# A transformer stage on one core: head pairs on row tiles of TensorE, projections by products of short parts, and a fixed order for each engine

## The chip, the cores and the metric

The kernel runs on one core of one Trainium2 chip. A core has five engines that run side by side, each through its own list of instructions in a fixed order, and synchronised by semaphores: TensorE (matrix products; PE in the profile, its weight loads PEld), VectorE (DVE), ScalarE (ACT), GpSimd (POOL), and SyncE (SP), which here issues all DMAs. The metric is the time of one execution in microseconds (us).

## The reference, cut to what matters

The kernel computes six blocks on `x` (4 x 256 x 256): cross attention, convolutional attention, a local transformer, cross attention, gated linear attention, and a mixture of experts. The change touches the third, a transformer of 6 layers whose attention looks back at most 64 tokens:

```python
DIM, DEPTH, HEADS, DIM_HEAD, WINDOW, INNER = 256, 6, 16, 64, 64, 1024
def attn_layer(x, Wqkv, qs, ksc, Wo):
    q, k, v = jnp.split(x @ Wqkv, 3, -1)                     # then split into 16 heads of 64
    q = l2norm(q) * qs
    k = l2norm(k) * ksc
    q = q * cos * scale + rotate_half(q) * sin * scale
    k = k * cos * inv + rotate_half(k) * sin * inv
    out = local_attention(q, k, v)                           # softmax(8 q k) v, j <= i <= j + 64
    return out @ Wo
def ffn_layer(x, g, bln, W1, b1, W2, b2):
    xn = (x - mu) / jnp.sqrt(var + 1e-05) * g + bln
    a, gate = jnp.split(xn @ W1 + b1, 2, -1)
    return a * jax.nn.gelu(gate, approximate=False) @ W2 + b2
for i in range(DEPTH):                                       # shift_tokens: half of the features one token later
    x = attn_layer(shift_tokens(x), Wqkv[i], q_scale[i], k_scale[i], Wo[i]) + x
    x = ffn_layer(shift_tokens(x), ln_g[i], ln_b[i], W1[i], b1[i], W2[i], b2[i]) + x
```

## The kernel before, in words

Each block is a stage (`Cross`, `Conv`, `Local`, `Gated`, `Experts`). The stage `Local` works on jobs: job j = 4 l + b is layer l of batch b, 24 in all, each with 256 tokens as two tiles of 128. A job has three parts, made as generators of steps:

- `front`: `features` (transpose the shifted x, L1803), then for q and k (sec 0 and 1), two tiles and two halves of 512 columns `proj` (L1811, two four-byte products), `sumsq` and `norm` (square on ScalarE L1612, sums on VectorE L1698, the power -1/2 on GpSimd L1579), the rotation on VectorE (L1684 to L1688) with an addition on GpSimd (L1572), `scale_k` (L1714), `turn` (transpose q or k, L1823, copied by ScalarE L1622 to L1626), and `values` (L1831, copied by L1631).
- `back`: attention by the class `Attention`, head by head. `front` there adds the mask (L965) and the scores (L967) in one bank for both query tiles; VectorE takes row maxima (L1005) and scales them (L1009), ScalarE the exponentials (L1038), VectorE (L1016, L1019) and GpSimd (L1026) divide; `turn` transposes the weights (L979 and L977, the latter a product with 64 output rows), ScalarE copies them (L1045); `apply` multiplies a pair of heads with the values (L990, two column tiles of 64), copied by L1476. q is kept twice, with zeros in the rows of the other head, so that 128 rows are multiplied. Then `wo` (L1855).
- `gated`: the feed-forward part, `fs`, `f_stats`, `f_scale`, `ft` (L1862), `w1` (L1871) with `gate` (ScalarE L1644, VectorE L1765), `w2` (L1881).

`order` interleaves the front of job n, the back of job n-1 and the gated part of job n-2 by `even`, which spreads each evenly over the same number of ticks. The one resulting list, `plan`, is the order of all five engines: each walks through it and does its own share of every step. Banks: 2 for scores, 2 for transposed weights, 1 for apply, 3 taken in turn by the steps `features`, `proj`, `turn`, `values`, `wo`, `ft`, `w1`, `w2`; TensorE waits for a bank of the three until its last user is copied out (`lt_gen_free`). The weights of q and k have two buffers, so a layer's are loaded during the layer before it.

In the stage `Experts`, products of four-byte numbers are made differently: each operand is split into a high part of short precision and the rest (type fp32r), and three products, high x high, high x low, low x high (`PARTS`), stand for one (L2414, L2429). In `Cross` the scores of two heads use two row tiles (L844, L856: 50 and 48 rows at rows 0 and 64).

## Time and profile before

| | |
|---|---|
| three runs | median 5052.75 us (5047.61 to 5063.53) |
| the profiled execution | 5055.65 us, span 5053.7 us |
| granted TensorE clock, mean | 0.970 |
| TensorE busy | 4552.4 us, 90% |
| VectorE, ScalarE, GpSimd busy | 3254.5, 2900.7, 1877.3 us |
| stage `Local` | about 1337 to 3337 us of the span |

A group or timeline row names line, engine, operation, output<-inputs, the shapes, and how many (x). A product of full four-byte numbers leaves two records in the trace, one of short parts a single record. A matmul's duration includes the time until its result is out, so what it costs in a row of others is read from start to start. "idle before <-" tells what ended an engine's idle time; "issue" is time for which the profile shows no cause.

### The profile page before, as it was taken

What the parts mean: (1) busy time and instruction counts of PE and PEld (TensorE: products, weight loads), DVE (VectorE), ACT (ScalarE), POOL (GpSimd) and SP (SyncE); (2) the same over time, 40 slices, a digit from 0 to 9 for tenths busy, and PEclk for the clock granted to TensorE, in tenths of its full rate; (3) what the DMA queues carried; (4) which work ended last, traced back from release to release, by engine and by line L of the source; (5) the groups of instructions that cost most, each with busy time, mean ns of one, the idle gap of its engine ahead of it and who ended that gap; (6) DMA issues with size and microseconds to landing.
All of it is one profiled execution on the core that took longest, in us unless ns stands there. A gap on an engine that the chain in (4) does not pass through costs nothing. (4 is left out here: it accounts for less than half of the span.)

```text
span 5053.7 us, 86339 instructions
## 1 busy us (share of the span) xinstructions
PE 4552.4 (90%) x32008; PEld 3054.5 (60%) x32008; DVE 3254.5 (64%) x7543; ACT 2900.7 (57%) x5798; POOL 1877.3 (37%) x1876
## 2 busy tenths in 40 slices
PE   5889998989699999999999999948999999759999
PEld 3555555547456666666666666635555555448888
DVE  5677777767565655656565565536777777575555
ACT  3666666668455656566565665615666666523332
POOL 3222232125454544445454444313222222025554
PEclk8999999999899999999999999979999999879999
DMA  6655555400200010100101000046556555111110
GB/s 136 128 102 106 106 113 107 77 23 1 70 23 15 24 33 12 53 13 14 44 12 53 5 23 24 4 98 136 111 102 113 107 106 89 24 49 48 47 48 22
DMA packets 189934, 305.64 MB, mean 60 GB/s; under 512 B 19736, under 2 KB 109752, under 8 KB 187832
## 3 DMA queue, kind: packets, MB, share of 16 engines
q1 hardware_dynamic: 189520, 300.13, 27.1%
q8 instruction: 259, 4.24, 0.4%
q14 instruction: 155, 1.27, 0.1%
HBM read 215.81 MB, written 73.40 MB: 57 GB/s over the span
## 5 line engine op out<-in xcount | busy, mean ns | idle before, releaser
L707 DVE TENSOR_REDUCE xa_m_part<-xa_ring 128x1 f32<-128x512 f32 x2048 | 1319.4, 686 | 505.8 <-PE xa_ring L856 491.5
L633 ACT ACTIVATE xa_ex<-xa_sc 128x1024 f32<-128x1024 f32 x1024 | 991.6, 1022 | 109.8 <-PE xa_sc L844 95.0
L856 PE MATMUL xa_ring<-xa_ks,xa_q_base 48*128 48x512 f32 x2048 | 517.8, 497 | 183.2 <-DVE xa_m_part L707 129.7
L870 PE MATMUL xa_pv<-xa_ex,xa_vs 128*17 128x256 f32 x8192 | 549.4, 386 | 4.2 <-issue 4.2
L856 PEld LDWEIGHTS xa_ring<-xa_ks,xa_q_base 48*128 48x128 f32 x2048 | 200.9, 185 | 515.3 <-DVE xa_m_part L707 433.6
L1572 POOL TENSOR_TENSOR lt_r_qk<-lt_r_qk,lt_t_rot 128x512 f32<-128x512 f32 x192 | 243.5, 1269 | 695.1 <-DVE lt_t_rot L1688 691.2
L1038 ACT ACTIVATE lt_p<-lt_bank,lt_stat,lt_rq 128x128 f32<-128x128 f32 (+1 forms) x768 | 366.2, 482 | 216.4 <-DVE lt_stat L1009 211.2
L844 PE MATMUL xa_sc<-xa_q_base,xa_ks 50*128 50x256 f32 x4096 | 423.1, 302 | 26.8 <-ACT xa_k L605 5.8
L844 PEld LDWEIGHTS xa_sc<-xa_q_base,xa_ks 50*128 50x128 f32 x4096 | 347.1, 187 | 117.4 <-ACT xa_vs L620 24.4
L1026 POOL TENSOR_SCALAR lt_p<-lt_p,lt_stat 128x192 f32<-128x192 f32 x384 | 339.9, 889 | 203.4 <-DVE lt_stat L1016 203.4
L2414 PE MATMUL moe_bank<-moe_xp,moe_wp 128*128 128x512 f32 x1536 | 373.3, 392 | 5.9 <-POOL moe_wp L2242 4.2
L1811 PE MATMUL lt_bank<-lt_wqk,lt_xt 128*128 128x512 f32 x768 | 366.2, 600 | 0.7 <-ACT lt_xt L1605 0.7
L555 POOL CAST xa_kp<-xa_k 128x512 fp32r<-128x512 f32 (+1 forms) x144 | 85.3, 592 | 653.3 <-ACT xa_k L613 311.7
L1579 POOL TENSOR_TENSOR lt_nrm<-lt_nrm,minus_half 128x16 f32<-128x16 f32 x96 | 280.5, 2922 | 122.6 <-DVE lt_nrm L1705 121.5
L2414 PEld LDWEIGHTS moe_bank<-moe_xp,moe_wp 128*128 128x128 f32 x1536 | 281.5, 189 | 59.9 <-issue 4.3
L870 PEld LDWEIGHTS xa_pv<-xa_ex,xa_vs 128*17 128x17 f32 x8192 | 189.1, 97 | 202.0 <-issue 62.7
L1612 ACT ACTIVATE lt_t_sq<-lt_bank 128x512 f32<-128x512 f32 x192 | 114.7, 597 | 296.2 <-DVE lt_t_rot L1688 296.2
L2277 ACT ACTIVATE moe_sg<-moe_bank 128x512 f32<-128x512 f32 x128 | 76.5, 598 | 341.1 <-PE moe_bank L2414 341.1
L979 PE MATMUL lt_bank<-ident,lt_p 128*128 128x128 f32 x768 | 240.5, 313 | 34.5 <-issue 34.5
L1871 PE MATMUL lt_bank<-lt_ft,lt_w 128*128 128x256 f32 x1152 | 262.1, 381 | 1.2 <-DVE lt_ft L1753 1.2
L2248 POOL TENSOR_TENSOR moe_hp<-moe_hh,moe_hp 128x512 fp32r<-128x512 f32 x128 | 166.0, 1297 | 256.9 <-ACT moe_hp L2255 256.9
L1005 DVE TENSOR_REDUCE lt_stat<-lt_bank 128x1 f32<-128x128 f32 (+1 forms) x768 | 210.7, 316 | 52.6 <-PE lt_bank L967 52.4
(283 smaller groups left out, 8962.8 us busy)
## 6 DMA issues: line engine op xcount, KB each, us to landing
xa_ks<-keys SPq DMA_DIRECT2D x384, 256.0 KB, 9.3
keys<-xa_kp SPq DMA_DIRECT2D x128, 512.0 KB, 3.8
xa_cx<-in_ctx_t SPq DMA_DIRECT2D x64, 512.0 KB, 4.6
lt_wqk<-in_lt_wqkv SPq DMA_DIRECT2D x6, 2048.0 KB, 9.0
lt_w<-in_lt_w SPq DMA_DIRECT2D x6, 1536.0 KB, 7.1
xa_q_base<-xa_m_rows SPq DMA_DIRECT2D x512, 2.0 KB
moe_w<-in_moe_wg SPq DMA_DIRECT2D x64, 128.0 KB, 2.1
moe_w<-in_moe_wu SPq DMA_DIRECT2D x64, 128.0 KB, 2.3
```

What stands on the lines that cost most here:

```text
L633: act.activation(x.ex[:, n % x.NE, :, :], x.sc[n % 2][:, :, :], ACT.Exp).then_inc(*x.ex_done.one())
L707: dve.tensor_reduce(x.m_part[:, i % 2, qt, h, ch:ch + 1], x.bank(n + odd), AX.X, ALU.max).then_inc(*x.dve_out.one())
L844: mm = pe.matmul(x.sc[n % 2][:, 2 * odd + pair, :], x.ks[unit % x.NU][rows, 2 * (g % 2) + pair, kt * P:(kt + 1) * P], x.q_base[rows, 2 * g ...
L856: pe.matmul(x.bank(n + odd), x.q_base[rows, pair, b * S + qt * P:b * S + (qt + 1) * P], x.ks[unit % x.NU][rows, pair % 4, ch * 512:(ch + 1 ...
L870: mm = pe.matmul(x.pv[32 * j:32 * j + x.VW, :], x.vs[:, i % x.NV, kt, 4 * g + j, :], x.ex[:, n % x.NE, 2 * (j % 2) + j // 2, :], start=(kt ...
L1026: pool.tensor_scalar(sv, sv, self.stat[:, n % 5, 3, 1:2], None, ALU.mult).then_inc(*self.div_pool.one())
L1038: act.activation(self.p[:, n % 5, at], s[:, at], ACT.Exp, bias=t3[:, 1, q:q + 1], scale=st.scale_of(b, h, slice(q, q + 1)) if st.scale is ...
L1572: pool.tensor_tensor(out, out, self.t_rot[:, t, :], ALU.add).then_inc(*self.rot_add.one())
L1579: pool.tensor_tensor(n[:, 2, :], n[:, 1, :], c.minus_half[:, 0:H], ALU.pow).then_inc(*self.rnorm.one())
L1811: mm = pe.matmul(bank[:, :], self.xt[:, par, k, tile * P:(tile + 1) * P], self.wqk[:, l % 2, k, col:col + 512], start=(k == 0), stop=(k == ...
L1871: mm = pe.matmul(bank[:, gate * S:(gate + 1) * S], self.w1[:, k, gate * FFP + m * P:gate * FFP + (m + 1) * P], self.ft[:, k, :], start=(k ...
L2414: mm = pe.matmul(self.banks[2 * (n % 2) + j][:, :], self.wp[:, wpart, i, j, k * FI:(k + 1) * FI], self.xp[:, xpart, k, at], start=(m == 0) ...
```

## The change

- Attention by a new class `Band`, on pairs p of heads. The scores of the even head use rows 0 to 63, of the odd one rows 64 to 127 (`st.q[rows, ...]`), so q is kept once, without zeros. The mask has 384 columns. Three banks for scores (of which a pair takes two), one for transposed weights, one for apply. Maxima of a head come from one instruction, scale and reciprocal of a pair from one.
- Projections and values by `PARTS`, six products in place of two. The weights come in 6 chunks of 512 columns (`raw`), are copied by ScalarE and subtracted by VectorE (`split`), into single buffers `wqk`, `wval`; the features are split in the same way.
- The attention of all jobs is one run of pairs: the transposes (`set_keys`) of a pair stand two pairs behind its scores, apply three, across jobs. `values` and `wo` stand together after the third pair. The gated part is that of job n-3.
- ScalarE, VectorE and GpSimd no longer follow `plan`. `order_of` sorts the steps for each of them by when TensorE reaches them by a table (`PE_TIME`), plus a delay (`LATER`), but before the step that needs them.

Core of the diff:

```diff
+    def pe_front(self, pe, on, st, p):
+        for odd in range(2):
+            on.wait_ge(self.exp_done, 2 * (2 * p + odd - 3) + 2)
+            pe.matmul(self.scores(2 * p + odd)[:, 0:2 * self.BLOCK], self.c.ident_bf[:, :], st.mask[:, :],
+                      start=True, stop=False)
+        j, hp = divmod(p, H // 2)
+        for q in range(2):
+            for odd in range(2):
+                rows = slice(64 * odd, 64 * odd + 64)
+                at = slice(self.BLOCK * q, self.BLOCK * q + self.KEYS[q])
+                mm = pe.matmul(self.scores(2 * p + odd)[:, at], st.q[rows, j % 2, hp, q * P:(q + 1) * P],
+                               st.kt[rows, j % 2, hp, self.FIRST[q]:self.FIRST[q] + self.KEYS[q]],
+                               start=False, stop=(q == 1))
...
+    def pe_turn(self, pe, on, n):
+        on.wait_ge(self.div_dve, 2 * (n // 2) + 2)
+        on.wait_ge(self.div_pool, n // 2 + 1)
+        on.wait_ge(self.t_out, n)
...
-    scale = None
+    PE_TIME = dict(features=0.5, proj=1.5, values=1.5, turn=0.5, attend=1.0, set_keys=0.6, apply=0.6, wo=3.4,
+                   ft=0.5, w1=1.7, w2=2.6)
...
-            self.at = Attention(c, "lt", ctx, (self.banks[0:2], self.banks[2:4], self.banks[4]), 4, 2, 1, WINDOW)
+            self.at = Band(c, "lt", ctx, self.banks[0:3], self.banks[4], self.banks[3])
...
+    def order_of(self, engine):
...
+        for step in self.plan:
+            key = ends[step] + self.LATER[engine].get(step[0], 0.0)
+            rank = self.RANK.index(step[0]) if step[0] in self.RANK else len(self.RANK)
+            for need in self.needed_by(step):
+                if need in begins:
+                    key = min(key, begins[need] - 0.01 * (len(self.RANK) + 1 - rank))
+            keys[step] = key
+        return sorted(self.plan, key=lambda step: keys[step])
...
-        for n in range(len(jobs) + 2):
-            parts = [(part(*jobs[n - lag]), steps, late) for lag, (part, steps, late) in
-                     enumerate(((self.front, 24, 0), (self.back, 23, 0), (self.gated, 17, 0.1)))
-                     if 0 <= n - lag < len(jobs)]
+        for n in range(len(jobs) + 2):
+            parts = [(part(*jobs[n - lag]), steps, 0) for lag, part, steps in
+                     ((0, self.front, 20), (1, self.back, 38), (3, self.gated, 21))
+                     if 0 <= n - lag < len(jobs) - (lag != 1)]
...
+            elif kind == "split":
+                n, = a
+                _, parts, last = self.chunk(n)
+                on.wait_ge(self.raw_in[n % 2], n // 2 + 1)
+                if n >= self.CHUNKS:
+                    on.wait_ge(self.gen_full, self.use[last] + 1)
+                act.activation(parts[:, 0, :, :], self.raw[:, n % 2, :, :],
+                               ACT.Copy).then_inc(*self.w_high.one())
...
-                    mm = pe.matmul(bank[:, :], self.xt[:, par, k, tile * P:(tile + 1) * P],
-                                   self.wqk[:, l % 2, k, col:col + 512], start=(k == 0), stop=(k == KC - 1))
+                    for xpart, wpart in PARTS:
+                        mm = pe.matmul(bank[:, :], self.xt[:, par, xpart, k, tile * P:(tile + 1) * P],
+                                       self.wqk[:, wpart, k, col:col + 512], start=(m == 0),
+                                       stop=(m == 3 * KC - 1))
+                        m += 1
```

TensorE before, at the start of a job's attention: L965 is a mask, L967 scores, L1811 a projection; bank0 and bank1 hold scores.

```order
L965 MATMUL lt_bank0<-lt_mask,ident_bf 128x320 [waits at_exp_done,lt_rq_done,lt_gen_free2]
L967 MATMUL lt_bank0<-lt_kt,lt_q_even 128x128
L967 MATMUL lt_bank0<-lt_kt,lt_q_even 128x192
L1811 MATMUL lt_bank6<-lt_wqk,lt_xt 128x512 [waits lt_gen_free1]
L1811 MATMUL lt_bank6<-lt_wqk,lt_xt 128x512
L965 MATMUL lt_bank1<-lt_mask,ident_bf 128x320 [waits at_exp_done]
L967 MATMUL lt_bank1<-lt_kt,lt_q_odd 128x128
L967 MATMUL lt_bank1<-lt_kt,lt_q_odd 128x192
```

TensorE now, around the same place (L1391 to L1394 the transposes of one head's weights, L1328 masks, L1335 scores, L2034 a projection, line numbers of the changed kernel):

```order
L1391 MATMUL lt_bank4<-ident,lt_p 128x128 [waits at_t_out]
L1392 MATMUL lt_bank4<-ident,lt_p 64x128
L1394 MATMUL lt_bank4<-ident,lt_p 128x128
L1328 MATMUL lt_bank2<-lt_mask,ident_bf 128x384 [waits at_exp_done,lt_gen_free1,lt_gen_free0]
L1328 MATMUL lt_bank0<-lt_mask,ident_bf 128x384 [waits at_exp_done]
L1335 MATMUL lt_bank2<-lt_kt,lt_q 128x128
L1335 MATMUL lt_bank0<-lt_kt,lt_q 128x128
L1335 MATMUL lt_bank2<-lt_kt,lt_q 128x192
L1335 MATMUL lt_bank0<-lt_kt,lt_q 128x192
L2034 MATMUL lt_bank7<-lt_wqk,lt_xt 128x512 [waits w_low,lt_gen_free2]
L2034 MATMUL lt_bank7<-lt_wqk,lt_xt 128x512 x5
```

The products of the two heads alternate between two banks, the transposes of weights all go to the one bank4 and wait there for ScalarE's copy of the head before (at_t_out), and between transposes and the next pair no other work stands.

ScalarE now, in the same stretch (L1362 exponentials, L1400 copies of transposed weights, L1836 of apply, L1819 of a turn):

```order
L1400 ACTIVATE lt_pt<-lt_bank4 128x384 [waits at_t_full]
L1819 ACTIVATE lt_kt<-lt_bank7 128x4x128 [waits lt_gen_full]
L1362 ACTIVATE lt_p,lt_stat<-lt_bank0,lt_stat,lt_rq 128x128 [waits at_max_done]
L1362 ACTIVATE lt_p,lt_stat<-lt_bank0,lt_stat,lt_rq 128x192
L1362 ACTIVATE lt_p,lt_stat<-lt_bank1,lt_stat,lt_rq 128x128
L1362 ACTIVATE lt_p,lt_stat<-lt_bank1,lt_stat,lt_rq 128x192
L1836 ACTIVATE lt_ot<-lt_bank3 128x256 [waits at_pv_done]
L1400 ACTIVATE lt_pt<-lt_bank4 128x384 [waits at_t_full] x2
L1836 ACTIVATE lt_ot<-lt_bank3 128x256 [waits at_pv_done]
L1362 ACTIVATE lt_p,lt_stat<-lt_bank2,lt_stat,lt_rq 128x128 [waits at_max_done]
```

Four exponentials now stand together where there were two, with the copies before and behind them.

## Rows read from the trace of the kernel before

**Rows 1.** The page: each engine's busy time, its share of the span, instructions.
```profile
PE 4552.4 (90%) x32008; PEld 3054.5 (60%) x32008; DVE 3254.5 (64%) x7543; ACT 2900.7 (57%) x5798; POOL 1877.3 (37%) x1876
```
**Rows 2.** Busy time by stretch: stretch, length, engines (x records), clock, DMA share, GB/s.
```profile
1528.00:1606.00 78.00, 75.96 (x387) 51.10 (x387) 46.42 (x140) 49.38 (x125) 37.10 (x31) 1.00 0.02 6
...
1684.00:1762.00 78.00, 75.93 (x393) 50.89 (x393) 47.23 (x140) 47.50 (x120) 35.28 (x29) 1.00 0.07 20
```
**Rows 3.** Line 1803, features: durations min/median/max in ns, first and last start.
```profile
L1803 PE MATMUL lt_bank<-ident,lt_xs x48: 272/273/421, 1365.1 to 3144.3; 128*128 128x128 f32 x48
```
**Rows 4.** Waits of TensorE, 1336 to 3345 us: total us, times, longest.
```profile
PE lt_bank L979 <- issue: 34.5, 24, 1.5
```
**Rows 5.** Timeline of TensorE, 1760 to 1780 us: start us, us, instruction.
```profile
1763.41 1.88 PE L1811 MATMUL lt_bank<-lt_wqk,lt_xt 128*128 128x512 f32 x4
1765.13 0.30 PE L965 MATMUL lt_bank<-lt_mask,ident_bf 128*128 128x320 bf16 x1
...
1765.91 0.87 PE L990 MATMUL lt_bank<-lt_pt,lt_v 128*64 128x256 f32 x8
1766.71 0.33 PE L979 MATMUL lt_bank<-ident,lt_p 128*128 128x128 f32 x1
...
1767.50 0.60 PE L1823 MATMUL lt_bank<-ident,lt_r_qk 128*128 128x128 f32 x4
1767.93 0.30 PE L965 MATMUL lt_bank<-lt_mask,ident_bf 128*128 128x320 bf16 x1
1768.07 0.71 PE L967 MATMUL lt_bank<-lt_kt,lt_q_odd 128*128 128x128 f32 x4
1768.62 0.27 PE L979 MATMUL lt_bank<-ident,lt_p 128*128 128x128 f32 x1
...
1769.18 0.33 PE L979 MATMUL lt_bank<-ident,lt_p 128*128 128x128 f32 x1
1769.35 2.75 PE L1881 MATMUL lt_bank<-lt_w,lt_u 128*128 128x256 f32 x12
```
**Rows 6.** Expert stage: timeline of TensorE from 4700 us; the page's group.
```profile
4703.16 2.91 PE L2414 MATMUL moe_bank<-moe_xp,moe_wp 128*128 128x512 f32 x12
4705.91 1.59 PE L2429 MATMUL moe_bank<-moe_wp,moe_hp 128*128 128x256 f32 x12
...
L2414 PE MATMUL moe_bank<-moe_xp,moe_wp 128*128 128x512 f32 x1536 | 373.3, 392 | 5.9 <-POOL moe_wp L2242 4.2
```
**Rows 7.** Row tiles in cross attention: TensorE from 600 us; loads begun 603.11 to 603.13.
```profile
603.01 0.50 PE L856 MATMUL xa_ring<-xa_ks,xa_q_base 48*128 48x512 f32 x2
603.34 0.92 PE L844 MATMUL xa_sc<-xa_q_base,xa_ks 50*128 50x256 f32 x8
...
603.11 0.19 PEld L844 LDWEIGHTS xa_sc<-xa_q_base,xa_ks 50*128 50x128 f32 x2
```
**Rows 8.** ScalarE's groups, 1528 to 3144: busy us, mean ns; last, the wide exponential.
```profile
L1045 ACT ACTIVATE lt_pt<-lt_bank 128x384 f32<-128x384 f32 x325 | 160.0, 492 | 15.0 <-PE lt_bank L979 14.5
L1038 ACT ACT_TABLE_LOAD x61 | 78.3, 1283 | 1.1
L1626 ACT ACTIVATE lt_kt<-lt_bank 128x512 f32<-128x512 f32 x80 | 47.8, 597 | 64.9 <-PE lt_bank L1823 64.9
...
L633 ACT ACTIVATE xa_ex<-xa_sc 128x1024 f32<-128x1024 f32 x1024 | 991.6, 1022 | 109.8 <-PE xa_sc L844 95.0
```
**Rows 9.** Groups of VectorE and GpSimd in the same stretch.
```profile
L1005 DVE TENSOR_REDUCE lt_stat<-lt_bank 128x1 f32<-128x192 f32 x322 | 112.1, 348 | 0.0
L1714 DVE TENSOR_TENSOR lt_r_qk<-lt_r_qk,lt_nrm 128x1024 f32<-128x1024 f32 x41 | 50.0, 1219 | 0.0
L1579 POOL TENSOR_TENSOR lt_nrm<-lt_nrm,minus_half 128x16 f32<-128x16 f32 x81 | 236.7, 2922 | 110.1 <-DVE lt_nrm L1705 109.2
```
**Rows 10.** Timeline of ScalarE from 1767.4 us.
```profile
1770.34 0.46 ACT L1038 ACTIVATE lt_p<-lt_bank,lt_stat,lt_rq 128x128 f32<-128x128 f32 x1
1771.28 0.38 ACT L1476 ACTIVATE lt_ot<-lt_bank 128x256 f32<-128x256 f32 x1
```

More of the change, by code:

```diff
@@ L1362, in order @@
         put(("load_mask",))
-        put(("load_values", 0))
         put(("tables", 0))
+        for n in range(self.CHUNKS):
+            put(("split", n))
+            if n + 2 < self.CHUNKS:
+                put(("raw", n + 2))
         for n in range(3):
@@ L1596, in act @@
         on = Waits(act)
-        for step in self.plan:
+        for step in self.orders["act"]:
             kind, *a = step
@@ L1650, in dve @@
         normalise(c, dve, y, self.normed)
[L1651 removed]
+        for step in self.orders["dve"]:
             kind, *a = step
```

359 lines of the change are left out of this document (262 added, 97 removed).

## The prediction

> **What bounds the kernel now.** I read the page first: TensorE is busy 90% of the span, the next engine 64% [rows 1]. The change touches one stage, the local transformer, so I cut that stage into stretches of 78 us [rows 2]. The reader is to see the same line each time: TensorE busy 75.96 of 78 us at a granted clock of 1.00, VectorE, ScalarE and GpSimd at 45 to 50% or less. The stage handles 24 jobs (6 layers x 4 batches). The transposes of the features start at 1365.1 us for the first job and 3144.3 us for the last [rows 3], so a job takes 1779.2 / 23 = 77.36 us, and 2.04 of each 78 us is idle: 75.3 us of TensorE work and 2.0 us of waiting per job. The waits of TensorE [rows 4] say the same: the most that an instruction waits inside the steady part is 34.5 us in 24 pieces over 1900 us. So what TensorE has to do decides this stage, and the rest is the question whether the other engines can follow once TensorE has less to do.
>
> **Projections.** Twelve halves per job (8 for q and k, 4 for values), each now four records of a full four-byte product of 512 columns. They last 1.72 us start to start (1763.41 to 1765.13) [rows 5]. After, each is six products of short parts with 512 columns. The expert stage already does exactly this: twelve such records from 4703.16 to 4705.91, 2.75 us, 0.229 each [rows 6]; six are 1.375 us. Saved: 12 x 0.345 = 4.1 us per job. The expert stage keeps TensorE just as full, so I take this as the firm term (bounds: half a present record, 0.215, gives 5.2 us per job; the busy mean of the expert stage, 373.3 / 1536 = 0.243, gives 3.1).
>
> **Scores in pairs.** Before, one head costs 0.69 us: a mask of 320 columns, 0.14, then four records, 0.55 (1767.93 to 1768.07 to 1768.62) [rows 5]; a pair 1.38. After, both masks have 384 columns: 2 x 0.14 x 384/320 = 0.34. The four matmuls use 64 rows each, the even head on the upper half of the array, the odd on the lower. That such halves run at once the cross attention shows: two products of 512 columns on two row tiles are 0.33 us apart from the next group [rows 7], where one behind the other would be 2 x 0.229 = 0.46; and the two weight loads of the next group begin within 0.02 us. So I price both heads' products at the 0.55 of one. To this comes changing the way the array is divided. Its price stands in the trace where a transpose, a 64-column product and a transpose follow one another: 1768.62 to 1769.35, 0.73 us [rows 5]. Four plain transposes are 0.43, so two are 0.215, and the two 128-column records between them are 2 x 0.107; undivided this would be 0.43. Two changes cost 0.30. The pair front needs two more changes than it did (in and out): 0.34 + 0.55 + 0.30 = 1.19, against 1.38. Saved: 8 x 0.19 = 1.5 us per job. Bounds: if the tiles did not overlap, 0.34 + 1.10 + 0.30 = 1.74 (2.9 us per job lost); if changing cost nothing, 0.89 (3.9 gained). I stay at 1.19, since both pieces have a row.
>
> The Trainium skill speaks against this part: "TensorEngine Tiling (Array Packing)", section Key Properties, says that a change of the tiling mode drains TensorE. By that rule the front gains 1.5 us per job, without it 3.9; the 0.73 us row agrees with the rule.
>
> **The same work elsewhere.** Transposes of the weights (0.73 to 0.79 per head), apply (0.80 per pair), wo, w1, w2 and the turns keep their instructions. TensorE's work per job becomes 75.3 - 4.1 - 1.5 = 69.7 us.
>
> **What the other engines get.** ScalarE: 4 of 8 half-height q copies go (4 x 0.59), and the order now puts the three gates of a job together with no exponential between, so 2 table loads remain of 5.8 (61 before exponentials [rows 8] and one fewer before gates, in 1616 / 77.36 = 20.9 jobs): 3.8 x 1.28 us less. New are 6 weight copies of 128x1024 per layer at 1.02 us (the exponential of that size [rows 8]), 1.5 us per job. VectorE: per pair two reduces of 384 columns (0.284 + 0.348 for 320 as two, so 1.0 ns a column and about 0.54 each), one scale and one reciprocal instead of two each [rows 9]; its new weight subtractions (1.22 for 128x1024, 6 per layer) and the feature subtraction (0.69) are less than it saves. GpSimd: 8 multiplications of 384 elements instead of 16 of 192 at 0.89. In sum all three have less to do; hidden, unless order makes them late.
>
> **The waits that come instead.** The fronts are no longer spread over the job. The middle (values, w1, wo) holds 20 us and more without scores, while around it four to five pairs follow each other with almost nothing between: front 1.19, two transposes of weights 1.50, apply 0.80, a turn 0.43: 3.9 us of TensorE per pair. ScalarE in the same time: four exponentials, 1.88 (two are 0.94, 1770.34 to 1771.28 [rows 10]), two copies of 0.49 [rows 8], one of 0.38 [rows 10], one of 0.60 [rows 8]: 3.84 us. Two engines with equal load, each in a fixed order, cannot both be full. The transposes have one bank instead of two, so the second set of a pair waits for ScalarE's copy of the first, and in ScalarE's row (third piece of order) such copies stand ahead of and behind four exponentials. The score banks are three for two heads: the second mask of the next pair waits for the exponentials of the even head, which come 2 x 0.54 + 0.385 (scale) + 0.94 = 2.4 us after the front ends, against 2.7 us of other TensorE work. Walking three pairs with these durations I get 0.6 to 1.4 us of waiting in two pairs; I take 0.6 for each of five pairs, 3.0 us per job. One more: the last turn of k stands 8 us behind the last projection; its chain is rotation 1.5, square 0.6, sum 0.67, the power of GpSimd 2.92, scaling 1.22 [rows 9], 7 us bare, with one or two pairs of attention ahead of it on VectorE: 1.0 us. Idle per job 4.0 instead of 2.0.
>
> **The sum.** 69.7 + 4.0 = 73.7 us against 77.36: 3.66 x 24 = 88 us gained. A layer's first projections now wait for weights copied and subtracted after the last use of the old ones, 1.02 + 1.22 us with 8 us to cover: 1 us at each of 5 changes of layer, 5 lost. The beginning waits for the mask behind a weight load of 2 MB; 1 MB now: I allow 2 us gained, and the first projection waits instead for its split. The end waits for the last feed-forward part as before: it is now a full step behind, with another job's to cover it, but that job's work came from under the attention; nothing. Total 88 - 5 + 2 = 85 us gained. The profiled execution took 5055.65 us, 2.9 above the median of 5052.75, inside the spread of 5047.61 to 5063.53. From the median: 4968, rounded to 4970.
>
> **Rivals.**
> A. TensorE is followed in full: idle stays at 2.0 us per job or falls with engines in their own order. For it: all three have less to do, and the waits before are mostly single gaps of 1.5 us. 24 x 5.6 = 134 gained less 2: 4920; with idle near nothing 4890. Chance 0.17.
> B. No change: the waits take all but a little, idle 7 to 8 us per job (1 us in each of five pairs more than I think, mostly the chain of the k turn). 5040 to 5065. Chance 0.09.
> C. Slower. One mechanism: the single transpose bank. If the second transposes of every pair wait for a copy queued behind four exponentials, that is 1.88 + 0.49 less the 0.80 + 0.43 that TensorE has between: 1.1 us x 192 pairs = 219 lost against 134: 5052 + 85 = 5138. It decides from 134/192 = 0.7 us per pair. Against it: in the projection stretches 1.4 us more lies between. Chance 0.10.
> D. The row tiles do not overlap: 4.4 us per job worse than forecast, 4970 + 106 = 5076. The pair in [rows 7] speaks against it. Chance 0.03. The skill's page "TensorE: Matmul & The Clock Gate", section LDWEIGHTS, says a load costs by its columns, not its rows; by this, an estimate of 0.107 us for 128 columns and 0.86 us for eight loads one after another, the front would be 1.50 and the time 5030. The trace has two such loads begun within 0.02 us of each other [rows 7], so I give that no chance of its own.
> The forecast itself, 4925 to 5025: 0.61.
>
> Measuring tells 0.3% (15 us) from no change. Faster by more: 0.61 + 0.17, plus a sliver of B: 0.79. Within: 0.08. Slower: 0.13. The range 4900 to 5060 leaves out the slower cases and the best of A.
>
> **What would show it.** Six-product projections 1.37 us apart; a pair front of 1.19 us start to start; a job period of 73.7; TensorE busy some 95% of a steady stretch, its waits naming ScalarE's copy of the transposes and exponentials. A period of 71 or less is A, of 77 B. If the projections took over 1.5 us or the front over 1.4, or the engines' chains made TensorE idle over 6 us per job, the forecast is wrong.

## The result, and where the time went

The changed kernel takes 5170.6 us (median of 5169.8, 5170.6 and 5174.7; a fourth, disturbed run of 5779.35 is left out) against 5050.9 for the kernel before on the same chip: 1.0234 times as long, interval 1.0211 to 1.0258. The forecast was 4970, faster. It was wrong in sign, by 201 us.

The page of the profiled execution (5169.8 us) beside [rows 1]:

```profile
PE 4537.9 (88%) x32584; PEld 3120.7 (60%) x32584; DVE 3224.3 (62%) x6644; ACT 2744.2 (53%) x5644; POOL 1726.2 (33%) x1682
```

Every engine is less busy than before. The stretches of 78 us that answer to [rows 2], and one at a change of layer (third row); the last row is the stage, first features to last w2 (columns as in [rows 2]):

```profile
1528.00:1606.00 78.00, 71.22 (x394) 51.08 (x392) 41.41 (x94) 38.02 (x107) 28.68 (x22) 0.98 0.01 1
1684.00:1762.00 78.00, 70.57 (x402) 50.33 (x403) 43.67 (x97) 40.69 (x116) 29.90 (x22) 0.98 0.02 6
1606.00:1684.00 78.00, 67.62 (x356) 47.15 (x354) 43.09 (x94) 41.00 (x108) 25.36 (x19) 0.89 0.11 32
1360.00:3437.00 2077.00, 1865.45 (x10170) 1327.86 (x10171) 1107.49 (x2474) 1022.28 (x2839) 746.25 (x552) 0.94 0.08 25
```

The reader sees two losses at once. TensorE is idle 7 us of 78 where it was 2, and its clock is no longer 1.00: 0.98 in an ordinary stretch, 0.89 where a layer changes. The same stage before:

```profile
1363.00:3325.00 1962.00, 1883.50 (x9598) 1264.27 (x9598) 1135.39 (x3373) 1180.77 (x2995) 891.18 (x744) 0.99 0.08 25
```

From such records I made a ledger of the stage for every kernel of this study: TensorE's busy time, its idle time, and how long the granted clock was at 1.2 instead of 2.4 GHz. If that halves the speed, busy time less half of the slow time in which TensorE is busy is the work at full clock. In us:

| kernel | stage | busy | idle | at 1.2 GHz | busy in it | work at full clock |
|---|---|---|---|---|---|---|
| before | 1961 | 1884 | 77 | 34 | 20 | 1874 |
| changed | 2077 | 1867 | 210 | 241 | 198 | 1768 |
| e1_plan_order | 2685 | 2075 | 610 | 980 | 668 | 1740 |
| e2_f_early | 2026 | 1830 | 196 | 157 | 118 | 1771 |
| e3_filler | 2041 | 1898 | 143 | 135 | 97 | 1849 |
| e5_no_reload | 1974 | 1812 | 162 | 108 | 77 | 1773 |
| e6_two_t | 2107 | 1880 | 227 | 248 | 199 | 1780 |
| e8_spread | 1990 | 1821 | 169 | 124 | 94 | 1774 |
| e9_apply_later | 1912 | 1789 | 123 | 78 | 50 | 1764 |
| e10_tuned | 1868 | 1783 | 85 | 71 | 43 | 1762 |
| e11_one_head | 1861 | 1777 | 84 | 54 | 29 | 1763 |
| e4_before_short | 1926 | 1823 | 103 | 80 | 66 | 1790 |
| e7_full_proj | 2094 | 1915 | 180 | 143 | 99 | 1865 |
| e12_full_proj | 1953 | 1872 | 81 | 63 | 39 | 1852 |

The last column supports the assumption: the kernels from "changed" to e11 give TensorE the same instructions (e3 has 78 us of filler more), and it comes out at 1740 to 1780 (e3: 1771 without the filler) while the slow time runs from 54 to 980. By the Trainium skill, page "TensorE: Matmul & The Clock Gate", section Terms, the penalty is about the throttled time times the share of pulses withheld, half here. The column agrees only when the slow time in which TensorE idles is left out: with it, e1 would come out at 1585.

So the change did take 107 us of work from TensorE (4.4 us per job; 5.6 were forecast). It then lost 133 us to new idle time and 89 to the clock (half of 198 less half of 20): 116 us longer. The ledger is good to some 20 us either way, by the spread of its last column. Single jobs at a clock of 1.00 throughout show the work without it, from one start of features to the next (before, e12, e10; e12 undoes the projections, see below):

```profile
1864.31:1944.30 79.99, 77.95 (x402) 52.47 (x401) 47.79 (x142) 49.49 (x126) 37.12 (x31) 1.00 0.02 6
...
2012.20:2090.19 77.99, 76.99 (x402) 48.81 (x401) 45.65 (x104) 42.87 (x121) 30.79 (x23) 1.00 0.07 19
...
1744.97:1819.19 74.22, 73.21 (x427) 53.07 (x426) 42.87 (x102) 40.72 (x119) 30.89 (x23) 1.00 0.16 51
```

TensorE's waits, 1336 to 3460 us (total us, times, longest), beside [rows 4]:

```profile
PE lt_bank L2095 <- DVE lt_fs L1963: 70.0, 22, 3.3
PE lt_bank L2048 <- DVE lt_r_qk L1932: 43.8, 25, 7.6
...
PE lt_bank L1391 <- ACT lt_pt L1400: 29.1, 69, 1.9
...
PE lt_bank L1328 <- ACT lt_p L1362: 20.7, 33, 2.2
...
PE lt_bank L2058 <- DVE lt_u L1986: 14.6, 22, 1.0
```

The largest is one that the prediction does not have at all: the transposes ft of the feed-forward features wait 3.3 us in nearly every job. Timeline of TensorE, VectorE and GpSimd around one of them:

```profile
1894.46 0.87 PE L1408 MATMUL lt_bank<-lt_pt,lt_v 128*64 128x256 f32 x8
1898.60 0.63 PE L2095 MATMUL lt_bank<-ident,lt_fs 128*128 128x128 f32 x4 [3.26 <-DVE lt_fs L1963]
...
1900.15 2.87 PE L2058 MATMUL lt_bank<-lt_wval,lt_xt 128*128 128x512 f32 x6
```
```profile
1890.59 0.41 DVE L1954 BATCH_NORM_STATS2 lt_fst<-lt_fs 128x6 f32<-128x256 f32 x1
...
1895.39 0.87 DVE L1352 SCALAR_TENSOR_TENSOR lt_stat<-lt_stat,lt_rq 128x4 f32<-128x4 f32 x1
1896.18 0.67 DVE L1916 TENSOR_REDUCE lt_nrm<-lt_t_sq 128x8 f32<-128x512 f32 x1
1896.78 1.67 DVE L1963 TENSOR_SCALAR lt_fs<-lt_fs,lt_fmv,lt_frs 128x256 f32<-128x256 f32 x2
```
```profile
1890.76 2.91 POOL L1768 TENSOR_TENSOR lt_nrm<-lt_nrm,minus_half 128x16 f32<-128x16 f32 x1 [2.03 <-ACT lt_p L1362]
...
1894.10 0.91 POOL L1780 TENSOR_TENSOR lt_frs<-lt_frs,minus_half 128x2 f32<-128x2 f32 x1
1894.98 1.26 POOL L1761 TENSOR_TENSOR lt_r_qk<-lt_r_qk,lt_t_rot 128x512 f32<-128x512 f32 x1
```

The features had been loaded by 1873.6, but VectorE takes their statistics only at 1890.59, its place in its own order; GpSimd's power for them (L1780) stands behind the 2.91 us power of the norms (L1768); and VectorE's scaling (L1963) behind a rotation, a division, two reduces and a sum of squares. TensorE wanted the result at 1895.3. Right behind the wait the clock falls to 1.2 GHz, from 1900.2 to 1903.6: the values product at 1900.15 takes 2.87 us for six records, 1.66 at full clock.

### The profile page after: what moved, and what is told of

Its sections match the earlier page's. It is cut to its first block and busy times, and to the rows that moved or that the text cites. A ratio compares the mean times of both kernels' runs of the same rounds, so it can differ in the third digit from the quotient of the medians.

```text
span 5168.0 us, 85679 instructions
## 1 busy us (share of the span) xinstructions
PE 4537.9 (88%) x32584; PEld 3120.7 (60%) x32584; DVE 3224.3 (62%) x6644; ACT 2744.2 (53%) x5644; POOL 1726.2 (33%) x1682
## 3 DMA queue, kind: packets, MB, share of 16 engines
q14 instruction: 145, 1.19, 0.1%
## 5 line engine op out<-in xcount | busy, mean ns | idle before, releaser
L1761 POOL TENSOR_TENSOR lt_r_qk<-lt_r_qk,lt_t_rot 128x512 f32<-128x512 f32 x192 | 245.7, 1280 | 719.8 <-DVE lt_t_rot L1906 719.4
L1362 ACT ACTIVATE lt_p<-lt_bank,lt_stat,lt_rq 128x128 f32<-128x128 f32 (+1 forms) x768 | 362.0, 486 | 155.8 <-DVE lt_stat L1352 155.8
L2034 PE MATMUL lt_bank<-lt_wqk,lt_xt 128*128 128x512 f32 x1152 | 329.0, 422 | 17.5 <-DVE lt_xt L1873 15.9
L1384 POOL TENSOR_TENSOR lt_p<-lt_p,lt_stat 128x384 f32<-128x384 f32 x192 | 191.9, 1000 | 437.2 <-DVE lt_stat L1376 437.1
L1768 POOL TENSOR_TENSOR lt_nrm<-lt_nrm,minus_half 128x16 f32<-128x16 f32 x96 | 280.0, 2917 | 128.4 <-DVE lt_nrm L1923 83.5
L1347 DVE TENSOR_REDUCE lt_stat<-lt_bank 128x2 f32<-128x384 f32 x384 | 195.7, 551 | 199.9 <-PE lt_bank L1335 199.9
L1400 ACT ACTIVATE lt_pt<-lt_bank 128x384 f32<-128x384 f32 x384 | 191.4, 498 | 189.0 <-PE lt_bank L1394 186.0
L2034 PEld LDWEIGHTS lt_bank<-lt_wqk,lt_xt 128*128 128x128 f32 x1152 | 213.1, 194 | 76.3 <-issue 18.7
```

The costliest lines, as they stand in the source:

```text
L1347: dve.tensor_reduce(t[:, 0, odd, :].rearrange("p (q o) -> p q o", o=1), self.scores(2 * p + odd)[:, 0:2 * self.BLOCK] .rearrange("p (q k) ...
L1362: act.activation(self.p[:, n % (2 * self.NP), P * q:P * q + self.KEYS[q]], self.scores(n)[:, self.BLOCK * q:self.BLOCK * q + self.KEYS[q]] ...
L1761: pool.tensor_tensor(out, out, self.t_rot[:, t, :], ALU.add).then_inc(*self.rot_add.one())
L1768: pool.tensor_tensor(n[:, 2, :], n[:, 1, :], c.minus_half[:, 0:H], ALU.pow).then_inc(*self.rnorm.one())
L2034: mm = pe.matmul(bank[:, :], self.xt[:, par, xpart, k, tile * P:(tile + 1) * P], self.wqk[:, wpart, k, col:col + 512], start=(m == 0), sto ...
```

## The experiments

Line numbers in rows are those of each kernel's own text; the names of the tiles stay.

**e1_plan_order.** Own orders off.

```diff
-        self.orders = {engine: self.order_of(engine) for engine in ("act", "dve", "pool")}
+        self.orders = {engine: self.plan for engine in ("act", "dve", "pool")}
```

> The changed kernel, with ScalarE, VectorE and GpSimd taking the steps in TensorE's order instead of an order of their own. Theory 1 (the loss comes from the orders themselves: they put what TensorE needs next, above all the normalised features of the feed-forward part, too late): the wait of the ft transposes, 3.3 us in 22 jobs, gets shorter and the time falls to 5090 to 5150 us. Rival 2 (the own orders are a help, and what costs is the new plan of the work with its dense attention): each rotation, exponential and transposed copy now stands exactly at its plan place, waits grow by 2 to 5 us per job, and the time rises to 5220 to 5300. I lean to rival 2 (0.6).

Measured 5784.0 us, 1.1437 (1.1410 to 1.1465) of before. Rival 2, and far beyond its range. Waits of TensorE, 1336 to 3460 us (over the whole stage, which here ends at 4053, they are 389.8 and 161.7):

```profile
PE lt_bank L1391 <- ACT lt_pt L1400: 312.7, 121, 7.6
PE lt_bank L2095 <- DVE lt_fs L1963: 124.4, 17, 8.0
```

The new plan does not stand without orders of their own. I took it from this that what is wrong lies in single places of them; e8 to e10 bear it out.

**e2_f_early.** Statistics and scaling of the features one slot earlier.

```diff
         put(("fs", l, b))
         yield ()
         yield ()
-        yield ()
         put(("f_stats", l, b))
         yield ()
         yield ()
         put(("f_scale", l, b))
         yield ()
+        yield ()
         put(("ft", l, b))
```

> The changed kernel, with the statistics and the scaling of the feed-forward features put one slot (of about 3.9 us) earlier in the plan; the transposes ft stay where they are, and TensorE's order is the same row for row. Theory 1 (waits for this chain, 70 us in 22, and the half clock that follows each of them decide a good part of the loss): the wait at ft goes nearly to nothing, the half-clock stretches behind it too (34 stretches of 184 us in all), and the time falls by 70 to 150 us, to 5020 to 5100. Rival 2 (the waits only move: the next step in line, the gelu or the transposed copies, is late by the same amount): below 30 us gained, 5140 or more, with the wait now at w2, the values or the weight transposes.

Measured 5119.1 us, 1.0119 (1.0095 to 1.0144) of before: 51 us under the changed kernel, short of the 70 expected. A stretch, waits, and two rows of the timeline:

```profile
1840.00:1918.00 78.00, 72.72 (x421) 51.99 (x419) 44.55 (x101) 39.79 (x114) 30.21 (x23) 1.00 0.11 33
```
```profile
PE lt_bank L1391 <- ACT lt_pt L1400: 57.3, 68, 1.9
...
PE lt_bank L2095 <- DVE lt_fs L1963: 28.5, 21, 1.5
```
```profile
1886.70 0.63 PE L2095 MATMUL lt_bank<-ident,lt_fs 128*128 128x128 f32 x4 [1.35 <-DVE lt_fs L1963]
...
1902.11 1.66 PE L2058 MATMUL lt_bank<-lt_wval,lt_xt 128*128 128x512 f32 x6 [0.65 <-DVE lt_u L1986]
```

The wait at ft fell by 41 us, but 28 came back at the copy of the transposed weights (29.1 to 57.3): in VectorE's row the statistics (at 1796.22) now stand ahead of the reduces (1797.50) that ScalarE's exponentials need (1799.67, after 3.28 us of waiting). Idle fell by only 14 us (210 to 196). The larger part is the clock: 84 us less at 1.2 GHz, 80 of them busy, worth 40. The clock does not fall behind every wait: jobs of this kernel with 5.2 and 6.9 us of idle time stay at 1.00 throughout. Both theories hold a part: the waits moved as rival 2 says, the clock came back as theory 1 says.

**e3_filler.** Work in place of the wait.

```diff
             elif kind == "ft":
+                for _ in range(19):
+                    pe.matmul(bank[:, 0:2 * Band.BLOCK], c.ident_bf[:, :], self.mask[:, :], start=True, stop=True)
                 on.wait_ge(self.f_scaled, 2 * j + 2)
```

> The changed kernel, with 19 products of the 384-column mask (0.16 us each, 3.0 us) put on TensorE ahead of the wait of the ft transposes, into the bank that ft then overwrites. It adds work where there was waiting (3.3 us in 22 jobs) and takes nothing away, so it tells what the clock costs apart from the wait. Theory 1 (the half clock behind this wait costs real time, about 1.7 to 3 us per job): the granted clock stays at 1.00 behind ft and the time falls by 30 to 75 us, to 5100 to 5140. Rival 2 (the half-clock stretches lie where TensorE would wait for others anyway, or the clock falls for another reason): the time stays within 15 us of 5170 or rises by up to 20 where the filler is longer than the wait.

Measured 5145.8 us, 1.0173 (1.0150 to 1.0197) of before: 25 us faster than the changed kernel with 3.2 us more work in every job.

```profile
1806.95 3.26 PE L2093 MATMUL lt_bank<-lt_mask,ident_bf 128*128 128x384 bf16 x19
1810.19 0.66 PE L2097 MATMUL lt_bank<-ident,lt_fs 128*128 128x128 f32 x4
```
```profile
1840.00:1918.00 78.00, 75.53 (x433) 53.88 (x432) 43.97 (x99) 40.78 (x117) 30.81 (x23) 1.00 0.10 33
```

Time at 1.2 GHz in the stage fell from 241 to 135 us. The fall of the clock behind a wait thus costs real time, apart from the wait. The gain is a little under the 30 expected.

**e4_before_short.** The kernel before with TensorE's side of the short parts alone.

```diff
-                for k in range(KC):
-                    mm = pe.matmul(bank[:, :], self.xt[:, par, k, tile * P:(tile + 1) * P],
-                                   self.wqk[:, l % 2, k, col:col + 512], start=(k == 0), stop=(k == KC - 1))
+                for m in range(3 * KC):
+                    mm = pe.matmul(bank[:, :], self.xt[:, par, m // 3, tile * P:(tile + 1) * P],
+                                   self.xt[:, par, :, :].rearrange("p k s -> p (k s)"), start=(m == 0),
+                                   stop=(m == 3 * KC - 1))
```
(the values likewise; xt is declared as short parts)

> The kernel before, with one part of the change alone: each of the 12 projection halves of a job as six products of short four-byte parts of 512 columns instead of two full four-byte products. It leaves out the split into parts and the weights: both sides of the product are the features, scaled by 0.01, so it prices TensorE's side alone. By the measured start-to-start times (1.72 before, 1.50 in the changed kernel) 12 x 0.22 = 2.7 us per job go, 63 us in 24 jobs. Theory 1 (TensorE bounds the kernel before, other engines have room): 4980 to 5000 us, a job period of 77.3. Rival 2 (the other engines' chains take it back as soon as TensorE has less to do, as in the changed kernel): 5030 to 5055, the idle time of TensorE up by 2 us or more per job, with half-clock stretches.

Measured 5027.2 us, 0.9941 (0.9921 to 0.9961) of before. 84 us of work are gone (3.4 per job at full clock, more than the 2.7 expected), but idle rose by 26 us and the slow time by 46: the stage is 35 us shorter, and only 25 us arrive, since the stages behind it take some 11 longer, which no run took up. That is rival 2, somewhat milder. TensorE's timeline just before the clock falls, which it does from 1642.3 to 1645.7:

```profile
1636.12 0.31 PE L965 MATMUL lt_bank<-lt_mask,ident_bf 128*128 128x320 bf16 x1 [0.57 <-ACT lt_p L1038]
...
1639.32 0.31 PE L965 MATMUL lt_bank<-lt_mask,ident_bf 128*128 128x320 bf16 x1 [0.22 <-ACT lt_p L1038]
...
1641.83 0.30 PE L979 MATMUL lt_bank<-ident,lt_p 128*128 128x128 f32 x1 [1.65 <-issue]
...
1642.58 2.91 PE L1832 MATMUL lt_bank<-lt_xt 128*128 128x512 f32 x6
```

The kernel before already had a wait of that kind (1.5 us, [rows 4]) with the clock at 1.00 through the steady part. With shorter products it has two small ones ahead of it, and the clock falls in 13 of the 21 jobs.

**e5_no_reload.** e2_f_early without the weight work of layers 1 to 5.

```diff
             if more:
-                for i in (n, n + 1):
-                    put(("split", first + i))
-                    put(("raw", first + i + 2))
...
-                on.wait_ge(self.w_low, self.CHUNKS * l + 2 * sec + half + 1)
+                on.wait_ge(self.w_low, 2 * sec + half + 1)
```

> The changed kernel with the feed-forward chain one slot earlier (the edit of e2_f_early, 5115 us in its profiled run), and without the loads, copies and subtractions of the projection weights of layers 1 to 5, which use those of layer 0: it leaves out these weights. In e2_f_early the two jobs at a change of layer take 82.8 and 85.0 us where the other two take 79.1 and 80.8. Theory 1 (the surplus comes from the six weight copies on ScalarE and the subtractions on VectorE that stand in the way of squares, exponentials and the k chain, and from the 17 us of half clock that follow): the jobs at a change of layer fall to 79 to 81, 8 us per change, 40 us in all: 5065 to 5085. Rival 2 (the surplus comes from the reload of the other weights or the tables, or moves to the next wait): less than 15 us gained, 5100 or more.

Measured 5064.4 us, 1.0015 (1.0002 to 1.0029) of before: 55 us less than e2_f_early. The jobs at a change of layer, by the starts of their features, fell from 82.8 and 85.2 us to 79.1 and 79.9. Theory 1 holds. A change of layer costs 11 us where the forecast allowed 1. The edit takes out the loads of the weights with the copies and subtractions, so it does not tell these apart.

**e6_two_t.** e2_f_early, banks dealt out differently.

```diff
-        return self.s_banks[n % 3]
+        return self.s_banks[n % 2]
...
-        on.wait_ge(self.t_out, n)
+        on.wait_ge(self.t_out, n - 1)
...
-            self.at = Band(c, "lt", ctx, self.banks[0:3], self.banks[4], self.banks[3])
+            self.at = Band(c, "lt", ctx, self.banks[0:2], (self.banks[2], self.banks[4]), self.banks[3])
```

> The changed kernel with the edit of e2_f_early, and with two banks for the transposed weights and two for the scores, in place of one and three. In e2_f_early TensorE waits 57 us in 68 pieces of at least 0.5 us for ScalarE's copy out of the single transpose bank, and 21 us in 33 for exponentials that free a score bank. Theory 1 (the single transpose bank is what makes TensorE wait inside the attention): these 57 us go, the waits for exponentials stay about the same, since already now the second mask of a pair waits for the even head of the pair before: 40 to 60 us gained, 5055 to 5075, with ordinary jobs near 77 us. Rival 2 (ScalarE is late as an engine: the same work comes one wait later, at apply or at the masks): the waits of L1391 go and those of the masks grow by as much, 5100 to 5130. Rival 3 (two score banks are too few): masks wait 0.5 us more in every pair, 96 us in all, 5140 or more.

Measured 5200.5 us, 1.0285 (1.0258 to 1.0313) of before: 81 us slower than e2_f_early.

```profile
PE lt_bank L1328 <- ACT lt_p L1362: 73.5, 124, 2.4
PE lt_bank L2096 <- DVE lt_fs L1964: 57.3, 22, 2.7
PE lt_bank L2049 <- DVE lt_r_qk L1933: 49.8, 25, 7.6
```

The waits for the transposed copy are gone from the list, and more has come elsewhere: at the masks (20.7 to 73.5) and at ft (28.5 to 57.3). Rival 3. I had argued that the third score bank hardly matters; taking it away costs more than a second transpose bank brings. Whether a second one helps with three score banks kept was not tried.

**e7_full_proj.** e2_f_early, projections undone.

```diff
-                    for xpart, wpart in PARTS:
-                        mm = pe.matmul(bank[:, :], self.xt[:, par, xpart, k, tile * P:(tile + 1) * P],
-                                       self.wqk[:, wpart, k, col:col + 512], start=(m == 0),
+                    mm = pe.matmul(bank[:, :], self.xt[:, par, 0, k, tile * P:(tile + 1) * P].bitcast(F32),
+                                   self.wqk[:, 0, k, col:col + 512].bitcast(F32), start=(k == 0),
```

> The changed kernel with the edit of e2_f_early, and with each projection half as two full four-byte products (of the high parts alone; it leaves out the low parts) in place of six products of short parts; copies and subtractions stay. It undoes TensorE's side of one part. The kernel before spent 1.72 us on such a half, the changed one 1.50: 12 x 0.22 = 2.7 us per job more work. Theory 1 (TensorE's work sets the time and waits are an addition to it): 45 to 65 us slower than e2_f_early, 5160 to 5185. Rival 2 (TensorE waits in the projection stretches for others, and longer products fill these waits and keep the clock up): within 20 us of e2_f_early, 5100 to 5140, with fewer half-clock stretches; then the short products earn next to nothing in this order.

Measured 5195.6 us, 1.0271 (1.0256 to 1.0287) of before: 76 us slower than e2_f_early, a little beyond theory 1. By the ledger 94 us of work.

**e8_spread.** e2_f_early; weight copies one at a time.

```diff
-        yield from round_robin(project(1, 0), turn(0, 1))
-        yield from project(1, 1)
-        weights(0)
-        yield from turn(1, 0)
-        weights(2)
+        for n, steps in enumerate(round_robin(project(1, 0), turn(0, 1))):
+            if n == 2:
+                weights(0)
+            yield steps
+        for n, steps in enumerate(project(1, 1)):
+            weights(1 + n)
+            yield steps
...
```

> The changed kernel with the edit of e2_f_early (5119 us), and with the four weight copies that e5_no_reload showed to cost most put one at a time between the projections and turns of the last job of a layer, the first one two slots earlier, instead of two and two behind the last projection. All the weights are loaded and split. e5_no_reload, without them, took 5064. Theory 1 (what a change of layer costs is the place of the copies in ScalarE's and VectorE's rows: two copies of 1.0 us and two subtractions of 1.2 at a stroke, behind which stand a square, the k chain and the exponentials): most of the 55 us come back, 5065 to 5090, the jobs at a change of layer at 79 to 81 us. Rival 2 (the work itself costs it, wherever it stands, or the wait for the load of the raw weights does): 5105 or more.

Measured 5091.7 us, 1.0070 (1.0053 to 1.0087) of before: 27 us of e5's 55 come back, with all the work done. Just outside theory 1's range; about half of the price is the place, the other half the work or its remaining places (e10 moves more of them).

**e9_apply_later.** e8_spread and two numbers.

```diff
-                     ((0, self.front, 20), (1, self.back, 38), (3, self.gated, 21))
+                     ((0, self.front, 20), (1, self.back, 38), (3, self.gated, 22))
-    LATER = dict(act=dict(attend=1.6, proj=1.9, gate=0.1),
+    LATER = dict(act=dict(attend=1.6, proj=1.9, gate=0.1, apply=0.9),
```

> e8_spread, and two more numbers of the order: ScalarE takes the copy of an attention output 0.9 us later in its row, so that the copy of the transposed weights, for which TensorE waits (57 us in 68 pieces in e2_f_early), stands ahead of it; and the feed-forward part of a job has 22 slots instead of 21. Nothing is added or left out. Theory 1 (the waits for the transposed copy are a matter of what stands ahead of it in ScalarE's row, not of the single bank): these waits fall by half or more, and with them the half-clock stretches; 40 to 70 us under e8_spread, 5000 to 5040, which is below the kernel before. Rival 2 (ScalarE has too much to do in the dense stretches, and a copy taken later is missed by the next apply): within 15 us of e8_spread, or slower, with waits now at the apply.

Measured 5006.6 us, 0.9911 (0.9896 to 0.9926) of before: 85 us under e8_spread, more than expected, and faster than the kernel before. Waits of TensorE:

```profile
PE lt_bank L1391 <- ACT lt_pt L1400: 44.3, 77, 1.4
...
PE lt_bank L1328 <- ACT lt_p L1362: 6.7, 6, 2.5
...
PE lt_bank L2100 <- DVE lt_fs L1968: 1.5, 1, 1.5
```

In e8_spread these are 62.1, 16.4 and 15.0. Waits for the transposed copy fell by a good quarter, not by the half I wrote; those at the masks and at ft fell by more. The 22 slots also move the feed-forward products in TensorE's own row, so the waits are not those of one order of TensorE. Which of the two numbers did more was not separated.

**e10_tuned.** Five more numbers.

```diff
-    LATER = dict(act=dict(attend=1.6, proj=1.9, gate=0.1, apply=0.9),
-                 dve=dict(attend=0.1, proj=0.1, sumsq=2.7,
+    LATER = dict(act=dict(attend=1.6, proj=1.9, gate=0.1, apply=0.9, split=0.4),
+                 dve=dict(attend=0.1, proj=0.4, sumsq=3.2, f_stats=1.6,
...
-            if b == B - 1 and l + 1 < DEPTH and i in (4, 5):
+            if b == B - 1 and l + 1 < DEPTH and i in (5, 6):
```

> e9_apply_later, and five more numbers of the order: VectorE takes the rotation 0.3 us, the sum of squares 0.5 us and the feature statistics 1.6 us later, ScalarE the weight copies 0.4 us later, and the last two weight copies of a layer stand one pair later. Theory 1 (TensorE's order is good and what is left of its waits lies in single places of the other rows): another 15 to 30 us less, 4975 to 5020, idle time of TensorE below 4 us per job. Rival 2 (these waits move, one instruction makes room for the next late one): within 10 us of e9_apply_later.

Measured 4960.5 us, 0.9819 (0.9804 to 0.9833) of before. Theory 1 holds, and the gain is beyond its range. A stretch, and the stage:

```profile
1684.00:1762.00 78.00, 76.99 (x451) 55.40 (x447) 46.34 (x109) 43.34 (x126) 33.15 (x25) 1.00 0.06 19
...
1352.00:3221.00 1869.00, 1782.11 (x10172) 1285.45 (x10173) 1078.09 (x2474) 1009.23 (x2839) 749.08 (x552) 0.98 0.09 28
```

TensorE is idle 1.4 us per job, the clock stays at 1.00 from 1472 to 3158 us, and a job takes 74.75 us in the mean against 80.00 before. The instructions are those of the changed kernel; only their order differs (TensorE's own by the 22 slots of e9, the other engines' by all the edits), and that is worth 210 us.

**e11_one_head.** e10_tuned; scores head by head.

```diff
-        for q in range(2):
-            for odd in range(2):
+        for odd in range(2):
+            for q in range(2):
```

> e10_tuned (4961 us, TensorE idle 1.4 us per job), with the four score matmuls of a pair in another order: both of the even head, then both of the odd, instead of even and odd by turns. In e10_tuned the records of even and odd start 0.007 us apart, and the scores of a pair take 0.75 us. Theory 1 (the halves of the array work at once only when neighbours in the row stand on different halves): of four steps only the middle pair still overlaps, so three steps instead of two, about 0.75 x 1.5 = 1.1 us; 8 x 0.37 x 24 = 70 us slower than e10_tuned, 5015 to 5045. Rival 2 (loads and products of the next half are taken up early enough in any order): within 10 us of e10_tuned.

Measured 4958.3 us, 0.9801 (0.9775 to 0.9827) of before: no change against e10_tuned. Rival 2. The eight score records of a pair still start in couples, now 0.014 us apart instead of 0.007, and take 0.756 us instead of 0.750 from the first start to the next group's. So the two halves of the array work at once in either order. The Trainium skill, page "TensorE: Matmul & The Clock Gate", section "The mechanism", says that TensorE pulls a weight load for other rows ahead of products in flight; these couples agree.

**e12_full_proj.** The edit of e7 on e10_tuned.

> e10_tuned with each projection half as two full four-byte products (of the high parts alone; it leaves out the low parts) in place of six of short parts; copies and subtractions stay. It prices the forecast's largest term, 4.1 us per job, in a kernel whose waits and half clock are nearly gone. In e7_full_proj the busy time of TensorE, with half of the half-clock time taken off, rose by 91 us, 3.8 us per job. Theory 1 (in e10_tuned TensorE sets the time): 85 to 100 us slower than e10_tuned, 5045 to 5060, so that without the short products all of the gain over the kernel before is gone. Rival 2 (the waits left over give some of it back): 60 us or less.

Measured 5053.2 us, 0.9990 (0.9975 to 1.0006) of before: 93 us over e10_tuned. Theory 1 holds. The stage:

```profile
1366.00:3319.00 1953.00, 1869.91 (x9593) 1179.95 (x9594) 1085.90 (x2474) 1015.90 (x2839) 746.75 (x552) 0.98 0.09 26
```

Without the short products the best order is as fast as the kernel before: they carry the gain.

## Why the prediction was wrong, step by step

**The base.** The period before is 80.00 us in every steady job, not the 77.36 of [rows 3]: the mean over 23 intervals had in it the first two, 36.4 and 63.1 us, in which the pipeline is filling. The first and the last row of a group give a mean, not a period. TensorE's work is then 77.95 us per job and not 75.3; the 2.0 us of idle time was right.

**Projections: near in sum, not in the working.** Forecast 4.1 us per job; e7 and e12 give 94 and 91 us of work, 3.9 and 3.8 per job. But six products take 1.48 to 1.50 us from start to start, and 1.57 to 1.68 behind w1 or w2, not 1.375, because the first of them stands 0.32 to 0.34 us ahead of the second behind a transpose, a turn, scores or apply, and 0.42 behind w1 or w2, where the others are 0.23 apart. Timeline of the changed kernel:

```profile
1886.24 1.66 PE L2034 MATMUL lt_bank<-lt_wqk,lt_xt 128*128 128x512 f32 x6
1887.74 0.27 PE L1391 MATMUL lt_bank<-ident,lt_p 128*128 128x128 f32 x1
```

Summed from start to start over the jobs at full clock, the projections and values of a job are 18.4 us in e10 and 21.1 in e12, 2.8 less. Most of the rest comes at wo, w1 and w2, 21.70 us against 22.45, whose instructions are the same and which the forecast took as unchanged. That the total was near is in part luck.

**Scores in pairs: the front right, the gain too high.** Forecast 1.19 us for a front, measured 1.17:

```profile
1847.59 0.49 PE L1328 MATMUL lt_bank<-lt_mask,ident_bf 128*128 128x384 bf16 x2
1848.01 0.82 PE L1335 MATMUL lt_bank<-lt_kt,lt_q 64*128 64x128 f32 x8
1848.76 1.56 PE L2114 MATMUL lt_bank<-lt_w,lt_u 128*128 128x256 f32 x6
```

Rival D is out. From start to start, masks and scores are 9.5 us per job in e12 where they were 11.6. But the transposes of weights and the turns, "the same work elsewhere", are 16.5 where they were 15.8, and other rows grew a little too. Against the kernel before, e12 keeps 0.9 us per job of TensorE's work (77.95 less 77.10, means over 20 jobs at full clock); 1.5 was forecast. The price that the forecast put on changing the division of the array, 0.15 us each time, no run separates as a whole. In e12 the first record of a full product stands 0.53 us ahead of the second behind scores or apply, and 0.43 behind a transpose or a turn: 0.10 there. By the Trainium skill, page "TensorE: Matmul & The Clock Gate", section LDWEIGHTS, the prediction had worked out 1.50 for the front; the trace has 1.17, so loads on the two halves do not add up here.

**The waits: the step that failed.** The forecast's "idle per job 4.0 instead of 2.0" came out as 7.1. Over the stage idle rose by 133 us where it had 48 plus a few: 102 in the 20 steady jobs, the rest in the first three. It put the new waits on ScalarE in the dense attention; the waits that TensorE has there (L1391, L1328) make 50 us of the list. What it left out is the chain of the feed-forward features, 70 us, and a wait of the values for a bank that the gate frees (L2058), 14.6, though its own argument held for them: a wait is made by what stands ahead in another engine's row. Its "1 us at each of 5 changes of layer" was 11 (e5). The wait at the last turn of k was seen, 1.0 us per job forecast, and 43.8 us measured, 1.8.

**The clock: not in the sum.** The forecast priced idle time at its own length, so the clock stood in it at nothing, without a reason. 89 us went to the clock, two thirds of the new idle time itself; e3 shows it apart from the waits. Waiting and clock together are 222 us against 107 us of work saved.

**Rivals.** A, idle time as before, is out. B wrote idle 7 to 8 us per job and 5040 to 5065: the idle time came, and the clock beside it. C came nearest in time (5138) and fails as a mechanism: its waits are 29 us in the changed kernel, not 219; e6, which removes them at the price of a score bank, is slower. Of the 201 us between forecast and result, some 82 are idle time, 89 the clock, and 27 work that did not go (107 instead of 134).

**What remains.** The forecast of 4970 lies near e10_tuned (4960.5), but not by its terms, and the nearness is luck. Per steady job e10 saves 4.6 us of work where 5.6 were forecast, and its idle time falls by 0.6 us (2.0 to 1.4) where it was to rise by 2.0. The end of the stage then takes part of this back. From the last features to the last w2 the changed kernel needs 218.5 us against 181.6 before (e10: 207.8), since the feed-forward part now runs three jobs behind; the first three jobs are 10 us shorter (e10: 14). "Nothing" was too little for that: of the 116 us by which the stage of the changed kernel is longer, the two ends make 27, and no experiment took it up.

## What to carry to other kernels

When TensorE gets less to do in a pipeline of fixed orders, follow for each thing that it waits for the whole row of the engine that makes it, the small statistics chains as well as the large copies; the loss sits where a short step stands behind a long one. Price an idle microsecond where the clock was at 1.00 higher than its length: here 133 us of new idle time brought 89 us of clock with it. It is no fixed price, since in e2_f_early jobs with 5.2 and 6.9 us of idle time lost nothing to the clock; read it from the granted clock of the stretch. And before giving up on a change that saves work, keep its instructions and move their places: 210 us lay there.

## What the runs showed of the hardware

VectorE and GpSimd hold each other up. The scaling of k (L1714 before, L1932 in the changed kernel), by durations min/median/max in ns:

```profile
L1714 DVE TENSOR_TENSOR lt_r_qk<-lt_r_qk,lt_nrm x48: 1217/1219/1234, 1384.7 to 3218.8; 128x1024 f32<-128x1024 f32 x48
```
```profile
L1932 DVE TENSOR_TENSOR lt_r_qk<-lt_r_qk,lt_nrm x48: 1217/1842/1850, 1397.1 to 3300.6; 128x1024 f32<-128x1024 f32 x48
L1352 DVE SCALAR_TENSOR_TENSOR lt_stat<-lt_stat,lt_rq x192: 161/164/981, 1422.3 to 3372.9; 128x4 f32<-128x4 f32 x192
```

Now 39 of 48 scalings of k fall together with GpSimd's division of the weights (L1384) and take 1.84 us instead of 1.22. Before, 24 of 48 fell together with that division too (L1026), and there it was GpSimd that was held up, 2.03 us instead of some 0.85, though it had started first:

```profile
1737.66 2.77 POOL L1026 TENSOR_SCALAR lt_p<-lt_p,lt_stat 128x192 f32<-128x192 f32 x2
...
1737.83 1.22 DVE L1714 TENSOR_TENSOR lt_r_qk<-lt_r_qk,lt_nrm 128x1024 f32<-128x1024 f32 x1
...
L1009 DVE SCALAR_TENSOR_TENSOR lt_stat<-lt_stat,lt_rq x384: 160/161/924, 1407.9 to 3274.4; 128x2 f32<-128x2 f32 x192
```

The change made the division a product of two tensors (TENSOR_TENSOR) where it was one with a scale per row (TENSOR_SCALAR); that this is why VectorE now waits there is likely, not shown. The scale of L1352 takes 0.16 us alone and up to 0.98 beside GpSimd's addition (L1761): the one at 1895.39 above ends at 1896.26, as GpSimd's addition of 1894.98 ends at 1896.24. Beside GpSimd's long power (L1768) it stays at 0.16, 45 times of 45. The reduces and rotations, which read PSUM, take the same beside GpSimd or alone (0.549 and 0.68 to 0.69 us). The Trainium skill, page "SBUF — State Buffer", section "SBUF: two separate sides", says that the port pair shared by the two is an exclusive lock, for VectorE instructions with two SBUF inputs among others, that whichever starts first has it for the whole instruction, and that the loser fully blocks. The end of L1352 agrees; the division of before, which started first and was held up, and the power, beside which L1352 does not wait, do not. The extra time of L1352, L1932 and L1963 is 84 us of VectorE in the stage, in chains whose end TensorE waits for. In the wait of 3.26 us above, L1352 took 0.87 us, and the two scalings of L1963 1.67 where the same two take 0.73 before (1737.18 us): 1.65 more. That sum is no loss of the change: before, the scale of L1009 alone had 82 us of it, 0.87 in place of 0.16 beside GpSimd's addition, 115 times. What is new is the place, at the scaling of k and of the feed-forward features. No run separated what this costs.
